# A mixture-of-experts layer behind a selective scan: the last shared block's start moved into the scan phase, the slot tables built in batches inside that block

## The chip, the cores and the metric

The kernel runs on one core of a Trainium2 chip. The metric is device microseconds of one execution, the median of several. Three runs of the kernel before gave 3494.13, 3504.29 and 3508.07 us. A core has TensorE (PE, with its weight load PEld), VectorE (DVE), ScalarE (ACT), GpSimd (POOL), SyncE (SP, which only issues DMAs here) and 16 DMA engines.

## The reference, cut to what matters

```python
x = x + layernorm(scan(layernorm(x)))          # 4096 rows of 512; softplus steps, state of 16
x = x + layernorm(moe(layernorm(x)))
def moe(xt):
    top_p, top_i = top_k(softmax(xt @ gate_w), 2)          # 8 experts
    for k in range(2):
        e, w = top_i[:, k], top_p[:, k]
        pos = (cumsum(one_hot(e), axis=0) - 1)[row, e]     # place of a token in its expert
        keep = pos < cap                                    # cap = 640
        buf[e, pos] = xt * keep
        y = gelu(buf @ w1 + b1) @ w2 + b2 + gelu(buf @ wd) @ wu
        out += y[e, pos] * keep * w
    return out + 0.2 * (gelu(xt @ sw1 + sb1) @ sw2 + sb2 + gelu(xt @ swd) @ swu)
```

Everything is in fp32. The large products run in the fp32r type, with each factor split into a high and a low part and three products (high-high, high-low, low-high) for one.

## The kernel before

The program has three phases with a barrier between them: `prepare` (projections and step sizes of the scan), `mix` (the scan), and `experts`.

In `mix` the work is placed by hand on a grid of units g, 64 per chunk of 512 rows, 8 chunks, and 64 more for the end (`END`). VectorE, ScalarE, GpSimd and TensorE each walk through all units and issue in each what is due then (`due(b, unit)` and the tuples `T_AT`, `X_HI_AT`, `X_LO_AT`, `UP_AT`, `DOWN_AT`). While the scan of a chunk runs, TensorE also does the shared expert of an earlier block of 512 rows: `turn` transposes four tiles of normalised rows, `x_hi` (ScalarE) and `x_lo` (VectorE) split them into `Xh` and `Xl`, up j=0 is the low-rank product with the logits in eight more columns, up and down of j=1 to 16 are the hidden layer in chunks of 128. `blocks(g)` yields the blocks that are under way, `FB` = 7 of the eight. In the 64 units after the scan only block 6's products are left. SP stores normalised rows (`xt_d`), logits (`lgT_d`) and the shared output.

`experts` has the eighth shared block (SB-1 = 7), and then eight experts of 10 tiles each, in blocks of 2, 4 and 4 tiles. A block is `run`: 17 chunks j, TensorE's order is up(j+1), a `turn` of the next block's tile at j in `FRONT`, extras, down(j). ScalarE applies GELU to up's result, VectorE makes its high part (`hh`, a copy) and low part (`hl`, a subtraction), down uses both. Beside it the next expert's weights come in: SP loads 256 KB pieces into a ring of four, ScalarE rounds them to the high part two chunks behind, when the old chunk's products are done, and GpSimd subtracts for the low part (`lows`, two operations a chunk), which frees the ring. The shared weights, split already in `mix`, are loaded by GpSimd in six `GROUPS` of four loads each; up(j) waits for its group.

Ahead of the shared block in `experts`, its rows are loaded, normalised, stored, turned and split one tile after another, the low-rank weights `L1` and `L2` are loaded and split again (`load_chunk(0, ...)`, `convert_chunk(0, 0)`, `lows(0, 0)`), and the logits of the first seven blocks are turned. The routing (softmax, two picks, cumulated counts by two products, places, table rows) runs on VectorE as `extra` steps in j = 1 to 12. After the block, `find_slots` fills the slot tables: for each of the 64 pairs (k, tile) VectorE makes a one-hot of the low 7 bits of the table row (128 columns) and one of the high bits times the token number (80 columns), and TensorE adds their product:

```python
v.tensor_scalar(low1[g % HOT], count_f[:, :], hl_f[:, 1, k, t:t + 1], None, ALU.is_equal)
v.tensor_scalar(high1[g % HOT], count_f[:, 0:E * ST], hl_f[:, 0, k, t:t + 1], tok_f[:, t:t + 1],
                ALU.is_equal, ALU.mult)
nc.tensor.matmul(psT[0][:, 0, 0:E * ST], low1[g % HOT], high1[g % HOT], start=(g == 0), stop=(g == K * NT - 1))
```

Then the table is copied, GpSimd gathers the first expert's two tiles of rows and its routing weights, TensorE turns them, and the first expert starts.

Of the kernel before, what the change touches and what calls it, by code (L numbers as in the profile page):

```python
# [24 lines left out]
P = 128  # L25
T, D = 4096, 512
NS, RANK = 16, 64
DT = D // P
# [342 lines left out]
W1_RING, W2_RING, HB_RING, HH_RING = 3, 3, 8, 4  # L371

# [6 lines left out]
def mix(nc, sem, const, early, x, dt_d, dtx_d, bc_d, xT_d, w, ws_d, lgT_d, x1_d, xt_d, sh_d):  # L379
# [6 lines left out]
    with ExitStack() as ctx:  # L386
# [13 lines left out]
        Xh, Xl = sb("Xh", [P, DT, CH], F32R), sb("Xl", [P, DT, CH], F32R)  # L400
        hh, hl = sb("hhs", [P, HH_RING, CH], F32R), sb("hls", [P, HH_RING, CH], F32R)
        L1h, L1l = sb("sL1h", [P, DT, P], F32R), sb("sL1l", [P, DT, P], F32R)
        L2 = sb("sL2", [L3, D], F32R)
# [3 lines left out]
        few = sb("b_few", [P, NU + FC + 14 * CT + 7 * CT])  # L407
# [34 lines left out]
        s_stat, s_pad, s_lhi, s_llo, s_l2 = (sem(f"b_{n}") for n in ("static_in", "pad", "low_hi", "low_lo", "low_up"))  # L442
# [33 lines left out]
        def blocks(g):  # L476

            return range(max(0, (g - FIRST) // NU - 3), min(FB, (g - FIRST) // NU))

# [9 lines left out]
        def _(sp):  # L489
# [63 lines left out]
            for g in range(END):  # L553
# [19 lines left out]
                if c > 0:  # L573
                    if k == 16:
                        store_x1(c - 1)
                    if c - 1 < FB and k in (20, 23, 29, 32):
                        store_xt(c - 1, (20, 23, 29, 32).index(k))
                for b in blocks(g):
                    for t in range(BT):
                        if due(b, OUT_AT) + 1 + t == g:  # L580
                            store_sh(b, t)
                    if due(b, UP_AT[0]) + 4 == g:
                        store_logits(b)
            sp.wait_ge(s_out, 16 * NCH)
            for q in range(2):
                sp.wait_ge(s_xt[q], FB * BT // 2 * 16)
            for t in range(BT):
                sp.wait_ge(s_sh[t], FB * 16)
            sp.wait_ge(s_lgs, FB * 16)

        @block.scalar
        def _(act):
# [94 lines left out]
            for g in range(END):  # L687
# [12 lines left out]
                if c > 0:  # L700
                    if k in (5, 6, 7, 8):
                        norm(c - 1, k - 5)
                    if c - 1 < FB and k in (18, 21, 27, 30):
                        norm_x1(c - 1, (18, 21, 27, 30).index(k))
                for b in blocks(g):
# [3 lines left out]
                    for j in range(J):  # L709
# [12 lines left out]
        def _(dve):  # L722
# [50 lines left out]
            def shared_out(b, t):  # L773
# [3 lines left out]
                if t >= 2:  # L777
                    dve.wait_ge(s_T, min(b + 2, FB) * BT)
                    dve.wait_ge(s_xt[t - 2], min(b + 2, FB) * (BT // 2) * 16)
# [15 lines left out]
            for g in range(END):  # L795
# [25 lines left out]
        def _(pool):  # L821
# [79 lines left out]
            nc.gpsimd.memzero(L1h[:, :, :]).then_inc(s_pad, 1)  # L901
            nc.gpsimd.memzero(L1l[:, :, :]).then_inc(s_pad, 1)
# [3 lines left out]
            for g in range(END):  # L906
# [14 lines left out]
                if 0 < c <= FB and k == 17:  # L921
# [8 lines left out]
        def _(pe):  # L930
# [28 lines left out]
            def up(b, j):  # L959
# [5 lines left out]
                else:  # L965
# [3 lines left out]
                    wh, wl = w1[n % W1_RING][:, 0, :, :], w1[n % W1_RING][:, 1, :, :]  # L969
                for d in range(DT):  # L970
                    for i, (a, v) in enumerate(((wh, Xh), (wh, Xl), (wl, Xh))):
                        last = nc.tensor.matmul(psH[:, :], a[:, d, :], v[:, d, :],  # L972
# [21 lines left out]
            for g in range(END):  # L994
# [4 lines left out]
                for b in blocks(g):  # L999
# [1143 lines left out]
```

## Time and profile before

| | us |
|---|---|
| median of three runs | 3504.29 |
| profiled execution | 3507.56 |
| its span | 3505.8 |
| TensorE busy | 3134.5 (89%) |
| VectorE, ScalarE, GpSimd busy | 1870.8, 1426.1, 1766.4 |
| TensorE's share of the chain that ended last | 53% |
| mean granted clock of TensorE | 0.935 |

A row of a timeline has a start, a duration, the engine, the line in the kernel and what was computed; matmuls are pipelined, so a single one lasts longer than the distance to the next. In square brackets stands how long the engine had been idle and who released it. The granted clock is 1.00 at 2.4 GHz and 0.50 at 1.2 GHz.

### The profile page before, as it was taken

How to read it: one execution, taken by the hardware profiler on the slowest of the kernel's cores; microseconds unless marked ns; L12 is line 12 of the kernel's file. 1: busy time of each engine (PE TensorE's matmuls, PEld its weight loads, DVE VectorE, ACT ScalarE, POOL GpSimd, SP SyncE). 2: the span in 40 equal slices, each digit the busy share in tenths (PEclk: the TensorE clock that was granted, in tenths of full speed). 3: DMA queues.
4: the chain of work that ended last, by engine and by line, in shares of the span. 5: the costliest groups of instructions: out<-in, count | busy, mean ns of one | idle time of the engine just before them, and what ended most of it. 6: DMA issues, size and time to landing. Idle time of an engine off the chain costs nothing.

```text
span 3505.8 us, 43215 instructions
## 1 busy us (share of the span) xinstructions
PE 3134.5 (89%) x15191; PEld 2569.3 (73%) x15191; DVE 1870.8 (53%) x2716; ACT 1426.1 (41%) x2522; POOL 1766.4 (50%) x1658
## 2 busy tenths in 40 slices
PE   6454698988989899689999999999999999999997
PEld 3233577777777777478888888888888888888886
DVE  6698989898898992373322322232223222322355
ACT  7555676666766764322231221321322312213232
POOL 1087797988878884342251341531522514405424
PEclk8655799999999999789999999999999999999999
DMA  7859687696977955821141230331322303304354
GB/s 256 250 173 239 180 238 207 198 259 192 249 194 219 244 174 168 263 85 40 43 102 22 69 79 16 97 64 19 112 36 55 90 19 79 76 10 108 79 181 153
DMA packets 279738, 467.63 MB, mean 133 GB/s; under 512 B 32321, under 2 KB 107985, under 8 KB 279522
## 3 DMA queue, kind: packets, MB, share of 16 engines
q1 hardware_dynamic: 211008, 274.60, 27.4%
q0 software_dynamic: 66752, 189.87, 20.8%
q8 instruction: 122, 2.00, 0.2%
q14 instruction: 94, 0.77, 0.1%
q10 hardware_dynamic: 1762, 0.40, 0.1%
HBM read 367.64 MB, written 97.14 MB: 133 GB/s over the span
## 4 chain that ended last, share of the span: by engine, by line
PE 53%; DMA 2%; DVE 2%; POOL 1%; issue 1%; ACT 1%; SPq 0%; POOLq 0%; DVEq 0%; ACTq 0%
PE c_psH L1959 26%; PE c_psY L2003 25%; PE c_psT L1950 1%; PE c_psT L2056 1%; DMA raw<-in_w 1%; PE c_psY L1999 0%; DMA out<-d_y 0%; DMA xrow<-x_d 0%; DVE yst L1673 0%; POOL W1l L1494 0%; DVE wgt L1850 0%; DVE hh L1683 0%; POOL W2l L1494 0%; ACT h L1409 0%; DVE hl L1684 0%
## 5 line engine op out<-in xcount | busy, mean ns | idle before, releaser
L1689 DVE CAST hh<-h 128x512 fp32r<-128x512 f32 (+1 forms) x400 | 180.4, 451 | 1178.0 <-ACT h L1415 1175.6
L829 POOL TENSOR_TENSOR u<-dtxs,Bt 128x512 f32<-128x512 f32 x512 | 669.6, 1343 | 162.7 <-DVE b_psA L732 148.9
L1415 ACT ACTIVATE h<-c_psH,biases 128x512 f32<-128x512 f32 (+1 forms) x400 | 248.2, 620 | 1222.1 <-PE c_psH L1959 1204.6
L732 DVE TENSOR_TENSOR_SCAN b_psA<-b_psA,b_few,u 128x512 f32<-128x512 f32 x512 | 657.0, 1283 | 58.8 <-ACT b_psA L602 55.7
L937 PE MATMUL b_psY<-ident,pr 128*128 128x128 f32 x2048 | 342.8, 305 | 221.8 <-DVE pr L739 202.4
L2003 PE MATMUL c_psY<-W2h,hh 128*128 128x512 f32 x1344 | 536.2, 399 | 4.3 <-DVE hl L1691 3.9
L2003 PE MATMUL c_psY<-W2l,hh 128*128 128x512 f32 x1344 | 527.0, 392 | 0.0
L2003 PE MATMUL c_psY<-W2h,hl 128*128 128x512 f32 x1344 | 525.8, 391 | 0.0
L1499 POOL DMA_INDIRECT xrow<-xt_d,slot_lists x80 | 91.1, 1139 | 817.9 <-PE c_psT L1950 417.1
L937 PEld LDWEIGHTS b_psY<-ident,pr 128*128 128x128 f32 x2048 | 262.3, 155 | 305.4 <-DVE pr L739 252.1
L739 DVE TENSOR_TENSOR pr<-b_psA,Ct 128x512 f32<-128x512 f32 x512 | 354.3, 692 | 20.4 <-DMA Ct<-bc_d 2.7
L602 ACT ACTIVATE b_psA<-dts,A_neg 128x512 f32<-128x512 f32 x512 | 354.3, 692 | 16.1
L1494 POOL TENSOR_TENSOR W1l<-raw,W1h 128x512 fp32r<-128x512 f32 x128 | 198.4, 1550 | 270.3 <-ACT W1h L1353 270.3
L972 PE MATMUL b_psH<-Xh,w 128*128 128x512 f32 x896 | 312.7, 410 | 9.8 <-DMA w<-ws_d 9.8
L2003 PEld LDWEIGHTS c_psY<-W2h,hh 128*128 128x128 f32 x1344 | 254.2, 189 | 57.2 <-DVE hl L1691 9.5
L991 PE MATMUL b_psS<-w,hhs 128*128 128x512 f32 x896 | 294.7, 411 | 0.0
L2003 PEld LDWEIGHTS c_psY<-W2h,hl 128*128 128x128 f32 x1344 | 253.7, 189 | 55.2
L2003 PEld LDWEIGHTS c_psY<-W2l,hh 128*128 128x128 f32 x1344 | 254.4, 189 | 46.9 <-issue 0.2
L1691 DVE TENSOR_TENSOR hl<-h,hh 128x512 fp32r<-128x512 f32 (+1 forms) x400 | 252.7, 632 | 13.8
L1959 PE MATMUL c_psH<-Xbh,W1h 128*128 128x512 f32 x576 | 224.7, 390 | 0.0
L1959 PE MATMUL c_psH<-Xbh,W1l 128*128 128x512 f32 x576 | 224.2, 389 | 0.0
L1959 PE MATMUL c_psH<-Xbl,W1h 128*128 128x512 f32 x576 | 224.1, 389 | 0.0
(278 smaller groups left out, 5792.7 us busy)
## 6 DMA issues: line engine op xcount, KB each, us to landing
w<-ws_d POOLq DMA_DIRECT2D x224, 512.0 KB, 6.7
raw<-in_w SPq DMA_DIRECT2D x256, 256.0 KB, 2.7
Bt<-bc_d SPq DMA_DIRECT2D x64, 512.0 KB, 15.1
Ct<-bc_d SPq DMA_DIRECT2D x64, 512.0 KB, 19.1
xn<-in_x SPq DMA_DIRECT2D x8, 1024.0 KB, 7.0
xT_d<-xnT SPq DMA_DIRECT2D x8, 1024.0 KB, 8.6
dt_d<-a_dt SPq DMA_DIRECT2D x8, 1024.0 KB, 7.2
dtx_d<-a_dx SPq DMA_DIRECT2D x8, 1024.0 KB, 7.6
```

Source lines behind the costliest of these rows:

```text
L602: nc.scalar.activation(psA[g % 2][:, :], dts[s % 2][:, :], ACT.Exp, scale=A_neg[:, s % DT, n:n + 1]).then_inc(s_dA, 1)
L732: nc.vector.tensor_tensor_scan(psA[q][:, :], psA[q][:, :], u[g % U_RING][:, :], carry[:, k:k + 1], ALU.mult, ALU.add).then_inc(s_h, 1)
L739: nc.vector.tensor_tensor(pr[g % PR_RING][:, :], psA[g % 2][:, :], C_of(g), ALU.mult)\
L829: nc.gpsimd.tensor_tensor(u[g % U_RING][:, :], dtx[s % 2][:, :], Bt[n // TG][:, n % TG, :], ALU.mult)\
L937: last = nc.tensor.matmul(psY[:, t, :], pr[g % PR_RING][:, t * P:(t + 1) * P], ident[:, :], start=(n == 0 and t == 0), stop=False, is_tran ...
L972: last = nc.tensor.matmul(psH[:, :], a[:, d, :], v[:, d, :], start=(d == 0 and i == 0), stop=(d == DT - 1 and i == 2))
L991: last = nc.tensor.matmul(psS[t][:, :], a, v, start=False, stop=(j == FC and i == 2))
L1415: nc.scalar.activation(h32[:, 0:n * P], psH[j % 2][:, 0:n * P], ACT.Gelu, bias=b1[:, j - 1:j]).then_inc(s_gelu, 1)
L1494: nc.gpsimd.tensor_tensor(lo, view, hi.bitcast(F32), ALU.subtract).then_inc(s_wlo, 1)
L1691: nc.vector.tensor_tensor(hl[j % 2][a], h32[a], hh[j % 2][a].bitcast(F32), ALU.subtract)\
L1959: last = nc.tensor.matmul(out, a, b, start=(i == 0), stop=(i == n - 1))
L2003: last = nc.tensor.matmul(psY[t][:, :], a[j % 2][:, c], b, start=False, stop=(j == J - 1 and i == 2))
```

## The change

The eighth block's rows are normalised, stored, turned and split in `mix`, in the 64 units behind the scan, and its up 0 is done there for the logits (`turned(g)`, one block further than `blocks(g)`). `Xh`, `Xl`, `L1` and `L2` are allocated once for both phases and stay; `L1` has 104 columns in `mix` too and is not cleared any more. `experts` starts with up 0 of the shared block; the bias and logits transpositions stand between up 0 and up 1 (`lead`). GpSimd issues the loads of the first two groups first, then its constants, then the other loads. The routing is spread over j = 0 to 7; the sums over tiles are one scan of 512 elements with resets in place of 16 scans of 32. The one-hots are built in eight batches of eight tiles by tensor_tensor operations into fp32r tiles, two batches in each of j = 8 to 11, and TensorE adds them in j = 9 to 12. The slots are found in j = 12; GpSimd gathers the first expert's rows before its low parts of chunks 10 to 16, and TensorE turns them in j = 14 and 15 (`FRONT_0`). The weights of the routing are stored in j = 10.

```diff
+        def turned(g):
+            return range(max(0, (g - FIRST) // NU - 1), min(FB + 1, (g - FIRST) // NU))
...
-                    if c - 1 < FB and k in (18, 21, 27, 30):
+                    if k in (18, 21, 27, 30):
                         norm_x1(c - 1, (18, 21, 27, 30).index(k))
-                for b in blocks(g):
+                for b in turned(g):
                     for t in range(BT):
                         if due(b, X_HI_AT[t]) == g:
                             x_hi(b, t)
-                    for j in range(J):
+                    if due(b, UP_AT[0]) + 2 == g:
+                        hidden_out(b, 0)
+                for b in blocks(g):
+                    for j in range(1, J):
...
-            nc.gpsimd.memzero(L1h[:, :, :]).then_inc(s_pad, 1)
-            nc.gpsimd.memzero(L1l[:, :, :]).then_inc(s_pad, 1)
...
-                for b in blocks(g):
+                for b in turned(g):
                     for t in range(BT):
                         if due(b, T_AT[t]) == g:
                             turn(b, t)
+                    if due(b, UP_AT[0]) == g:
+                        up(b, 0)
+                for b in blocks(g):
                     for j in range(J):
-                        if due(b, UP_AT[j]) == g:
+                        if j > 0 and due(b, UP_AT[j]) == g:
                             up(b, j)
...
-FRONT = (2, 6, 10, 14)
-HOT = 4
+FRONT, FRONT_0 = (2, 6, 10, 14), (14, 15)
+BATCH = 8
+BATCHES = K * NT // BATCH
+BATCH_AT = 8
...
+        low1 = sb("low_one_hot", [P, 2, BATCH, P], F32R, rt)
+        high1 = sb("high_one_hot", [P, 2, BATCH, E * ST], F32R, rt)
...
+            for b in range(SB):
+                sp.dma_start(logits_in(b), lgT_d[:, b * BT * P:(b + 1) * BT * P]).then_inc(s_lin, 16)
             sp.dma_start(b2bc[:, :], w["sb2"].partition_broadcast(P)).then_inc(s_b2, 16)
-            sp.dma_start(graw[:, :, :], w["gate"].rearrange("(a p) e -> p a e", p=P)).then_inc(s_gin, 16)
-            for b in range(SB - 1):
-                sp.dma_start(old_logits(b), lgT_d[:, b * BT * P:(b + 1) * BT * P]).then_inc(s_lin, 16)
-            rows(SB - 1)
             sp.wait_ge(s_bt, 2)
-            load_chunk(0, SHARED_W, 0)
...
-            nc.scalar.activation(rs1[:, :], mv1[:, :, 1], ACT.Sqrt, bias=eps[:, :]).then_inc(s_sd, 1)
-            act.wait_ge(s_pad, 2)
-            act.wait_ge(s_gin, 16)
-            nc.scalar.copy(L1h[:, :, L3:L3 + E], graw[:, :, :]).then_inc(s_ghi, 1)
-            act.wait_ge(s_nm, 1)
-            for t in range(BT):
-                normalise(SB - 1, t)
-                x_hi(shared(SB - 1), 1, None, t)
 ...
-            run(shared(SB - 1), b1T[:, E * FC:], logits=True, wset=1, extra={2: (exponentials,)})
...
-            act.wait_ge(s_wst, K * 16)
-            for t in range(EB[0][1]):
-                x_hi(expert(0, 0), X_OF[0], None, t)
+            def store_weights():
+                act.wait_ge(s_wT, 1)
+                nc.scalar.copy(weight_rows, psT[1][0:K * NT, 0, :]).then_inc(s_wTc, 1)
+                act.wait_ge(s_wTc, 1)
+                for k in range(K):
+                    act.dma_start(w_d[k].rearrange("(r p) o -> r (p o)", p=P), weight_rows[k * NT:(k + 1) * NT, :])\
+                        .then_inc(s_wst, 16)
+            run(shared(SB - 1), b1T[:, E * FC:], nxt=(expert(0, 0), X_OF[0], None), front=FRONT_0, wset=1, extra={1: (exponentials,), BATCH_AT + 2: (store_weights,)})
...
+            for k in range(2):
+                load_shared(k)
+            nc.gpsimd.memset(wsl[:, :], SHARE).then_inc(s_share, 1)
...
+            nc.gpsimd.memset(fresh.rearrange("p (x t) -> p x t", t=NT)[:, :, 0:1], 0.0).then_inc(s_rc, 1)
+            for k in range(2, len(GROUPS)):
+                load_shared(k)
+            for j in range(BATCH_AT + 2):
                 lows(1, j)
-            for q in range(2):
-                pool.wait_ge(s_xts[q], BT // 2 * 16)
             slots_known(0)
             gathers(0, 0, range(2))
             pool.wait_ge(s_wst, K * 16)
             gather_weights(0, 0)
+            for j in range(BATCH_AT + 2, J):
+                lows(1, j)
             gathers(0, 1, range(2))
...
+            def sums():
+                step(v.tensor_tensor_scan(RA[:, :, :, :].rearrange(flat), fresh, RB[:, :, :, :].rearrange(flat), 0.0,
+                                          ALU.mult, ALU.add))
...
+            def one_hots(i):
+                k, r = i * BATCH // NT, slice(i * BATCH % NT, i * BATCH % NT + BATCH)
+                low, high = low1[:, i % 2, :, :], high1[:, i % 2, :, :]
+                def spread(a, n):
+                    return a.unsqueeze(2).to_broadcast([P, BATCH, n])
+                def counts(n):
+                    return count_f[:, 0:n].unsqueeze(1).to_broadcast([P, BATCH, n])
+                dve.wait_ge(s_rows, 1)
+                after(dve, s_add, i - 1)
+                v.tensor_tensor(high, counts(E * ST), spread(hl_f[:, 0, k, r], E * ST), ALU.is_equal).then_inc(s_heq, 1)
+                v.tensor_tensor(low, counts(P), spread(hl_f[:, 1, k, r], P), ALU.is_equal).then_inc(s_low, 1)
+                dve.wait_ge(s_heq, i + 1)
+                v.tensor_tensor(high, high.bitcast(F32), spread(tok_f[:, r], E * ST), ALU.mult).then_inc(s_high, 1)
             def find_slots():
-                dve.wait_ge(s_rows, 1)
-                for g in range(K * NT):
-                    k, t = g // NT, g % NT
-                    after(dve, s_add, g - HOT + 1)
-                    v.tensor_scalar(low1[g % HOT], count_f[:, :], hl_f[:, 1, k, t:t + 1], None, ALU.is_equal)\
-                        .then_inc(s_low, 1)
-                    v.tensor_scalar(high1[g % HOT], count_f[:, 0:E * ST], hl_f[:, 0, k, t:t + 1], tok_f[:, t:t + 1],
-                                    ALU.is_equal, ALU.mult).then_inc(s_high, 1)
-                dve.wait_ge(s_add, K * NT)
+                dve.wait_ge(s_add, BATCHES)
...
+            routing = {0: (less_max,), 2: (probabilities, lambda: pick(0)), 3: (lambda: mark(0),),
+                       4: (lambda: pick(1), lambda: mark(1)), 5: (totals, sums), 6: (places,), 7: (table_rows,)}
+            for i in range(0, BATCHES, 2):
+                routing[BATCH_AT + i // 2] = (lambda i=i: one_hots(i), lambda i=i: one_hots(i + 1))
+            routing[BATCH_AT + BATCHES // 2] = (find_slots,)
...
+            def biases_and_logits():
+                pe.wait_ge(s_bin, 32)
+                nc.tensor.transpose(psT[0][:, 0, :], raw[0][:, 0:P], ident[:, :]).then_inc(s_bt, 1)
+                nc.tensor.transpose(psT[1][:, 0, 0:FC], raw[1][0:FC, 0:P], ident[0:FC, 0:FC]).then_inc(s_bt, 1)
+                pe.wait_ge(s_lin, SB * 16)
...
+                last.then_inc(s_lT, 1)
...
-            run(shared(SB - 1), 1, 0, logits=True, extra={8: cumulate})
-            pe.wait_ge(s_rows, 1)
-            nc.tensor.transpose(psT[1][0:K * NT, 0, :], wgt[:, :, :].rearrange("p k t -> p (k t)"), ident[:, :])\
-                .then_inc(s_wT, 1)
-            for g in range(K * NT):
-                pe.wait_ge(s_low, g + 1)
-                pe.wait_ge(s_high, g + 1)
-                nc.tensor.matmul(psT[0][:, 0, 0:E * ST], low1[g % HOT], high1[g % HOT],
-                                 start=(g == 0), stop=(g == K * NT - 1)).then_inc(s_add, 1)
-            pe.wait_ge(s_wTc, 1)
-            for t in range(EB[0][1]):
-                turn(expert(0, 0), t)
+            def turn_weights():
+                pe.wait_ge(s_rows, 1)
+                nc.tensor.transpose(psT[1][0:K * NT, 0, :], wgt[:, :, :].rearrange("p k t -> p (k t)"), ident[:, :])\
+                    .then_inc(s_wT, 1)
+            def add_slots(i):
+                pe.wait_ge(s_low, i + 1)
+                pe.wait_ge(s_high, i + 1)
+                for o in range(BATCH):
+                    last = nc.tensor.matmul(psT[0][:, 0, 0:E * ST], low1[:, i % 2, o, :], high1[:, i % 2, o, :],
+                                            start=(i == 0 and o == 0), stop=(i == BATCHES - 1 and o == BATCH - 1))
+                last.then_inc(s_add, 1)
+            steps = {5: (cumulate,), BATCH_AT: (turn_weights,)}
+            for i in range(0, BATCHES, 2):
+                steps[BATCH_AT + 1 + i // 2] = (lambda i=i: add_slots(i), lambda i=i: add_slots(i + 1))
+            steps[FRONT_0[0] - 1] = (lambda: pe.wait_ge(s_wTc, 1),)
+            run(shared(SB - 1), 1, 0, lead=biases_and_logits, nxt=expert(0, 0), front=FRONT_0, extra=steps)
...
+            def kept_tile(name, shape, dt=F32R, where=ctx):
+                return where.enter_context(nc.sbuf_tensor(name, shape, dt, side="right"))
+            kept_tile("edge", [P, 16], F32)
+            const["L1"] = [kept_tile(f"L1{h}", [P, DT, L3 + E]) for h in "hl"]
...
+            const["L2"] = kept_tile("L2", [L3, D])
+            const["X"] = [kept_tile(f"X{h}", [P, DT, CH]) for h in "hl"]
```

## Rows read from the trace of the kernel before

**Rows 1.** Four stages: engines' busy us (count), granted clock, DMA share, GB/s.

```profile
1442.90:1539.10 96.20, 96.18 (x409) 77.39 (x409) 51.17 (x87) 35.44 (x60) 53.90 (x49) 0.97 0.79 240
1539.10:1580.40 41.30, 29.90 (x138) 28.64 (x137) 33.40 (x138) 2.68 (x6) 9.73 (x10) 0.56 0.12 35
1580.40:1631.80 51.40, 51.36 (x319) 46.73 (x320) 16.49 (x43) 11.41 (x23) 10.89 (x13) 0.95 0.16 51
1816.80:1868.70 51.90, 49.74 (x320) 44.70 (x319) 19.06 (x44) 12.76 (x26) 20.91 (x18) 1.00 0.33 67
```

**Rows 2.** The chain that ended last, in order of time: start us, us, what.

```profile
1458.13 2.72 PE c_psH L1959 x12
```

**Rows 3.** Timeline between the phases: start us, us, engine, line, operation.

```profile
1402.51 0.39 PE L991 MATMUL b_psS<-w,hls 128*128 128x512 f32 x1
...
1409.56 0.11 POOL L1545 MEMSET slot_lists<- 128x10 f32 x1 [11.44 <-POOLq L2124]
...
1414.92 0.59 POOL L1566 DMA_DIRECT2D W1h<-ws_d  x1
...
1442.82 0.75 POOL L1566 DMA_DIRECT2D W1h<-ws_d  x1
...
1453.86 0.80 POOL L1568 DMA_DIRECT2D W2l<-ws_d  x1
```

**Rows 4.** Timeline of TensorE, start of the shared block.

```profile
1442.92 0.76 PE L1959 MATMUL c_psH<-Xbh,L1h 128*104 128x512 f32 x1 [5.17 <-POOL L L1494]
...
1448.17 0.55 PE L1959 MATMUL c_psH<-Xbh,W1h 128*128 128x512 f32 x1
...
1452.52 0.39 PE L1959 MATMUL c_psH<-Xbh,W1h 128*128 128x512 f32 x1
```

**Rows 5.** Timeline of the scan phase: clearing a tile, turning a tile of rows.

```profile
171.51 0.53 POOL L901 MEMSET sL1h<- 128x512 uint32 x1
...
1256.31 0.60 PE L956 MATMUL b_psH<-ident,xn 128*128 128x128 f32 x4
```

**Rows 6.** DMA issues, from 1417 and from 1445.6 us: KB each, us to landing.

```profile
W2l<-ws_d POOLq DMA_DIRECT2D x2, 256.0 KB, 6.4
...
W2l<-ws_d POOLq DMA_DIRECT2D x1, 1024.0 KB, 15.0
```

**Rows 7.** Timeline of ScalarE and TensorE at the first converted chunk.

```profile
1466.71 0.62 ACT L1353 CAST W1h<-raw 128x512 fp32r<-128x512 f32 x1 [5.13 <-DMA raw<-in_w]
...
1468.68 0.68 ACT L1415 ACTIVATE h<-c_psH,biases 128x512 f32<-128x512 f32 x1
...
1471.57 0.39 PE L2003 MATMUL c_psY<-W2h,hh 128*128 128x512 f32 x1
```

**Rows 8.** VectorE groups with shapes, 1400 to 1600 us: count, busy us, mean ns.

```profile
L1808 DVE TENSOR_SCALAR xrow<-U,RA 128x128 f32<-128x128 f32 x64 | 18.5, 290 | 0.0
...
L1741 DVE TENSOR_TENSOR RB<-RB,w 128x256 f32<-128x256 f32 x2 | 0.9, 426 | 0.1
...
L1763 DVE TENSOR_TENSOR RA<-RA,RB 128x512 f32<-128x512 f32 x1 | 0.7, 684 | 0.0
```

**Rows 9.** Timeline of GpSimd and VectorE, a collision and a free pair.

```profile
1504.05 1.47 POOL L1494 TENSOR_TENSOR W2l<-raw,W2h 128x512 fp32r<-128x512 f32 x1
...
1504.41 1.66 DVE L1691 TENSOR_TENSOR hl<-h,hh 128x512 fp32r<-128x512 f32 x1
...
1523.57 0.43 DVE L1689 CAST hh<-h 128x512 fp32r<-128x512 f32 x1 [1.41 <-ACT h L1415]
1524.03 0.69 DVE L1691 TENSOR_TENSOR hl<-h,hh 128x512 fp32r<-128x512 f32 x1
```

**Rows 10.** Timeline of GpSimd and TensorE, the first expert's rows.

```profile
1572.76 1.16 POOL L1499 DMA_INDIRECT xrow<-xt_d,slot_lists  x1 [29.83 <-issue]
...
1577.77 1.12 PE L1950 MATMUL c_psT<-ident,xrow 128*128 128x128 f32 x4 [0.32 <-DMA xrow<-xt_d,slot_lists]
...
1590.07 0.60 PE L1950 MATMUL c_psT<-ident,xrow 128*128 128x128 f32 x4
```

More of the change, by code:

```diff
@@ L798, in _ @@
                     static_lo()
-                for b in blocks(g):
+                for b in turned(g):
                     for t in range(BT):
@@ L998, in _ @@
                         add_skip(g // NS)
-                for b in blocks(g):
+                for b in turned(g):
                     for t in range(BT):
@@ L1673, in leave, with run @@
                 nc.vector.scalar_tensor_tensor(out, psY[t][:, :], scale, out, ALU.mult, ALU.add).then_inc(s_yev, 1)
-            def run(at, logits=False, nxt=None, extra=None, late=None, leaves=True):
+            def run(at, nxt=None, extra=None, late=None, leaves=True, front=FRONT):
                 G, n = at["B"] * J, at["n"]
@@ L1961, in products, with run @@
                 return last
-            def run(at, xb, s, logits=False, nxt=None, extra=None, final=False):
+            def run(at, xb, s, lead=None, nxt=None, extra=None, final=False, front=FRONT):
                 G, n = at["B"] * J, at["n"]
@@ L1990, in down @@
                     if j == 0:
-                        if logits:
+                        if lead:
                             pe.wait_ge(s_lg, 4)
@@ L2009, in run @@
                 up(0)
+                if lead:
+                    lead()
                 for j in range(J):
@@ L2012, in run @@
                         up(j + 1)
-                    if logits and j == 0:
-                        pass_gate(pe, s_lT, at["B"] + 1, g_pe)
-                        for t in range(BT):
-                            last = nc.tensor.transpose(psH[0][:, t * E:(t + 1) * E],
-                                                       h32[L3:L3 + E, t * P:(t + 1) * P], ident[L3:L3 + E, L3:L3 + E])
-                        last.then_inc(s_lP, 1)
-                    if nxt and j in FRONT and FRONT.index(j) < nxt["n"]:
-                        t = FRONT.index(j)
+                    if nxt and j in front and front.index(j) < nxt["n"]:
+                        t = front.index(j)
@@ L2021, in run @@
                         turn(nxt, t)
                     if extra and j in extra:
-                        extra[j]()
+                        for part in extra[j]:
+                            part()
                     down(j)
-            for t in range(BT):
-                turn(shared(SB - 1), t)
-            pe.wait_ge(s_bin, 32)
-            nc.tensor.transpose(psH[0][:, 0:P], raw[0][:, 0:P], ident[:, :]).then_inc(s_bt, 1)
-            nc.tensor.transpose(psH[1][:, 0:FC], raw[1][0:FC, 0:P], ident[0:FC, 0:FC]).then_inc(s_bt, 1)
@@ L2059, in _ @@
-            for t in range(EB[0][1]):
-                turn(expert(0, 0), t)
+                pe.wait_ge(s_rc, 7 + E)
+                pe.wait_ge(s_b1, 2)
+                picked = OH[:, :, :, :].rearrange(flat)
+                nc.tensor.matmul(psT[0][:, :, :].rearrange("p a b -> p (a b)"), U[:, :], picked, start=True, stop=True)
+                nc.tensor.matmul(psT[1][:, :, :].rearrange("p a b -> p (a b)"), ones[:, :], picked,
+                                 start=True, stop=True).then_inc(s_cum, 1)
```

253 lines of the change are left out of this document (90 added, 163 removed).

## Prediction

> **What bounds the kernel now.** I read the chain of waits first. It is TensorE for half of the span, and inside the shared block and the expert blocks it is nothing else: twelve products take 2.72 us [rows 2], so a chunk j (one up, one down) takes 5.44 us, and every other engine waits for it. The two places where TensorE does not work are seen in the table of stages and in the timeline between the phases. The last product of the scan phase starts at 1402.51, the experts phase starts at 1409.56, and its first product only at 1442.92 [rows 3, 4]: the last shared block's rows are loaded, normalised, turned and split there first. After that block come 41.3 us [rows 1] in which TensorE is paced by VectorE: 64 pairs of one-hots, one pair per product, then the slots are copied, the first expert's rows gathered and turned, and at 1580.38 the first expert starts. The granted clock shows the same: 0.97 and 1.00 in the blocks, 0.56 in this gap. From there to the end TensorE is full (49.74 of 51.9 us even in a block with a boundary). So the change is worth what it removes between 1402.5 and 1580.4, less what it adds to TensorE or makes TensorE wait for.
>
> **The change, part by part.** S is the first instruction of the experts phase on GpSimd (1409.56 before); I count from it.
>
> 1. Start of the scan phase: two clearings of 0.53 us [rows 5] go, and they stand ahead of the first product for the scan on GpSimd. -1.0 (0 to -1.0).
>
> 2. End of the scan phase: eighth block. Its four tiles of rows are turned there (4 x 0.60 us [rows 5]) and the low-rank product with the logits done (2.72): +5.1 on TensorE, which is full there. ScalarE and VectorE get four normalisations, four high and four low copies, SP four row stores and one of logits; both engines mostly wait in this stretch, and the order by units places each turn one down product after the copies it waits for. I count no stall; a missed slot each time would be about 1 us, so +4.6 to +9. S becomes 1409.56 - 1.0 + 5.1 = 1413.7.
>
> 3. Start of the experts phase: loading, normalising, turning and the low-rank weights' loading are gone; weights and rows lie in SBUF. Up 0 starts at once, at the low clock: in the trace twelve products took 1442.92 to 1448.17 = 5.25 us and then the clock rose [rows 4]. What is late next is data. The biases and eight logits pieces must land (ten issues on SP, which feed 34 small transposes), and up 1 needs the first weights: their fourth issue is some 1.6 us after S, and such a load lands 6.4 us after issue [rows 6], so S+8. Up 1 takes 2.7 to 5.25 by the clock, down 0 another 1.0: the third up starts at S+11.7 to S+14.3. I take S+13.
>
> 4. Weight supply. GpSimd issues eight loads, about 3 us of constants (an estimate, those of before and two more), then sixteen loads (11.8 us before, 1442.82 to 1454.6 [rows 3]), so from S+7.3 to S+19.1. Before, the last load of the group for j=5 to 8 was issued at 1447.9 and took 15.0 us [rows 6], 20 us after the first of the sixteen: S+27.4. TensorE wants it after the third up plus six half chunks, S+13+16.3=S+29.3. No stall, with 1.9 us to spare. The expert's own chunks are tighter. Before, GpSimd was done with its issues 2.1 us after the third up's start; now 6.1 us after. It then had waited for ScalarE until 1458.2, so only some 1.5 us of the 4 come through. The first converted chunk waited 5.13 us for its load, the next GELU came at 1468.68, and the down product that uses it started at 1471.57 [rows 7]; the two VectorE steps between end about 0.4 us ahead. 1.5 - 0.4 gives +1.0 (0 to 3).
>
> 5. The routing and the batches. From the third up to the end of the block took 1452.52 to 1538.9 = 86.4 us [rows 4, 1], the two cumulating products included; that stays. The routing steps only move by some chunks, under the same cover. New on TensorE are 64 products of 128x80 in j=9 to 12. The trace has none in this type. By columns from 0.227 us for 512 it is 0.035 each, 2.3 in all; the nearest other, a 128x128 transposition, is 0.15 busy [rows 5], 9.6 in all. I take 0.09 each: +5.8. Two turns of the expert's rows inside: +1.0.
>
> VectorE now computes 8 batches of three operations, 640, 1024 and 640 elements. From 426 ns for 256 and 684 ns for 512 elements [rows 8] it is 168 ns + 1.01 ns per element: 0.81 + 1.20 + 0.81 = 2.8 us a batch, 5.7 us a chunk. Its own pair for the block is 0.43 + 0.69. But GpSimd makes two low halves per chunk, and while one runs, a VectorE operation with two SBUF inputs stands still: the low half of h took 1.66 us beside such a GpSimd operation and 0.69 without [rows 9]. That is 1 us per low half, 2 per chunk. VectorE's chunk is 1.1 + 5.7 + 2.0 = 8.8 us, TensorE's 5.44 + 1.45 = 6.9 us. Four chunks give 7.6 us; VectorE has about a half chunk of lead at the start. +6 (0 to 14). The double buffer doesn't bind: a batch waits for the product of the one two before it, which in the same chunk comes earlier.
>
> The Trainium skill ("SBUF — State Buffer", Who interferes with whom) says that a VectorE instruction with two SBUF inputs and a GpSimd instruction that reads SBUF exclude each other for the whole instruction. The trace agrees with 1.66 against 0.69 us [rows 9]. By full exclusion of the 2.6 us of two low halves the chunk would be 9.4 us and the forecast 2 us later, 3454.
>
> The skill's "VectorE: DVE Perf Modes" (The perf-mode tier table) speaks against this edit: a tensor_scalar in fp32 has a double rate from SBUF, a tensor_tensor has not, and the batches change from the one to the other. At 128 elements the trace shows 290 ns for tensor_scalar [rows 8], nearly all of it fixed, so per element the batch is the cheaper one here.
>
> 6. End of the shared block. Slots known just after the adds of j=12; 1572.76 to 1577.77 are 5.0 us from the first gather to the second tile's turning [rows 10], and turn 0 stands 11 us behind in TensorE's queue: hidden. But GpSimd now does the low halves of seven chunks (14 x 1.3 us) after these gathers, and behind them the gathers for the second block. Next in its queue stand row stores, weights and those gathers. The last low half needs the last down product, then some 4 us; gather and landing 3.5 us; TensorE turns that tile 9.7 us after the expert's start (1580.38 to 1590.07). +0.5 (0 to 5). The expert's first block then is like a later one with its boundary, 51.9 instead of 51.4 us [rows 1]: +0.5.
>
> **Sum.** Before, S to the expert's start: 1580.38 - 1409.56 = 170.8. After: 13 + 86.4 + 1.0 + 5.8 + 6 + 1.0 = 113.2. That is -57.6; with -1.0, +5.1 and +1.0 it is -52.5. The profiled execution has 3505.8 us of span and 3507.56 in all, 3.3 above the median of 3504.29. So 3455.1 by that execution, 3451.8 by the median: **3452 us**, 1.5% faster. All terms at their good end give 3439, all at their bad end (+25) 3477.
>
> **Rivals.**
> - VectorE decides more than I count: operands repeated along a dimension run at half rate. Nothing in the trace repeats both inputs of one operation. A chunk would be 1.1 + 11.3 + 2.0 = 14.4 against 6.9, 30 us instead of 6: 3476.
> - Weight supply. The shared weights are 16.8 MB; the block moved 240 GB/s on average [rows 1]. At that rate the 8.4 MB up to j=8 last 35 us and TensorE stands 6 us: 3458. Against it: 1024 KB loads then landed in 15.0 us with three others ahead of them.
> - The end of the block: GpSimd's queue, in which the second block's gathers stand behind 14 low halves, makes TensorE wait at the tile turned in j=2, or ScalarE's late conversions hold a GELU, 5 us: 3457. This is also how the change would not do all that it says.
> - The other side: the clock. TensorE now starts the block cold, with pauses for logits and weights. If these keep it at the lower level (0.437 us a product in up 0 against 0.227) through the block's 400 products, that is +84: 3536, slower than before. It decides if the clock is still 0.5 after j=3. Against it: it rose 5.25 us after the first product, and before that TensorE had been idle even longer.
>
> **How the numbers follow.** Forecast 0.68, VectorE 0.10, supply 0.09, block's end 0.08, clock 0.03, no gain for a reason I don't see 0.02. The range, 3439 to 3475, holds the forecast with its terms, the supply, the block's end and most of the first rival. A measurement of this kernel tells about 0.5% (17.5 us) from no change: faster 0.95 (everything up to 3487), within 0.02, slower 0.03.
>
> **What would show it.** Right: last product of the scan phase 4 to 5 us later; first product of the experts within 0.5 us of S; third up at S+13 and clock 1.00 from there; no TensorE wait at j=3 and j=5; chunks j=8 to 11 at 7 to 9 us with VectorE nearly full; no gap at the end of the block, and the first expert about 53 us earlier (near 1527); all later blocks as before. Wrong: a weights wait on TensorE, batches' operations above 1.5 us with GpSimd idle, a late clock, or a block of the experts that is longer than its 51.9 us.

## The result, and the profile after

| | before | changed | difference |
|---|---|---|---|
| time, median (range), us | 3504.36 (3494.13 to 3508.07) | 3459.52 (3457.46 to 3466.31) | ratio 0.988 (0.9855 to 0.9905) |
| span of the profiled execution, us | 3505.8 | 3455.7 | -50.1 |
| first expert's first product after S, us | 170.8 | 121.7 | -49.1 |

The forecast was 3452 with a range of 3439 to 3475; the kernel came out 7.5 us slower than forecast. The sign, the place and six sevenths of the gain (44.8 of 52.3 us) are right. The difference of the two spans, 50.1 us, holds 3.9 us that are the luck of the profiled execution (experiment 1). What the single parts bring is read from the profiles; only the last part, the early gathers, was also taken back by itself (experiment 4).

The stages of the changed kernel, columns as in [rows 1]: start to third up, to the batches, the batches, to the end of the block, the first expert's first block.

```profile
1409.30:1423.80 14.50, 11.26 (x63) 8.42 (x63) 3.09 (x10) 1.68 (x5) 14.41 (x37) 0.67 1.03 281
1423.80:1470.80 47.00, 46.22 (x199) 36.69 (x198) 33.04 (x51) 19.55 (x32) 24.24 (x22) 1.00 1.21 371
1470.80:1502.30 31.50, 30.01 (x150) 25.56 (x149) 28.58 (x30) 7.64 (x14) 8.91 (x6) 0.89 0.19 60
1502.30:1531.00 28.70, 24.56 (x106) 19.94 (x106) 14.88 (x16) 7.55 (x14) 18.21 (x16) 0.94 0.37 103
1531.00:1582.10 51.10, 49.48 (x319) 44.52 (x318) 18.64 (x44) 12.76 (x26) 16.14 (x17) 1.00 0.22 67
```

The 41.3 us at clock 0.56 of [rows 1] are gone, and so are the 33 us before the first product [rows 3, 4]. What is not as forecast is seen in lines three and four: the clock is 0.89 and 0.94 where it was 1.00, and in line four TensorE is busy 24.56 of 28.70 us. TensorE's timeline at the start, against [rows 4]; a bracket is idle time and what ended it:

```profile
1408.94 0.73 PE L1915 MATMUL c_psH<-Xh,L1h 128*104 128x512 f32 x1 [6.26 <-PEq L2097]
...
1416.91 0.63 PE L1985 MATMUL c_psY<-ident,OH 8*128 8x8 f32 x16 [3.24 <-DMA RB<-lgT_d]
...
1417.92 0.80 PE L1915 MATMUL c_psH<-Xh,W1h 128*128 128x512 f32 x1
...
1423.76 0.40 PE L1915 MATMUL c_psH<-Xh,W1h 128*128 128x512 f32 x1
```

S is 1409.32. The first product stands 0.4 us ahead of it, the logits land at S+7.6, up 1 starts at S+8.6 and takes 4.9 us, ten of its products at the low level (0.427 us apart), and the third up starts at S+14.4.

The chain of waits of the changed kernel, in its own order of time (start us, us, what). Of [rows 2] only TensorE stood there; now there are gaps between TensorE's stretches:

```profile
1420.77 19.53 DMA W2l<-ws_d
1440.34 3.04 PE c_psH L1915 x12
...
1486.56 1.91 DVE high_one_hot L1775
1488.47 1.83 DVE high_one_hot L1772
1490.37 0.99 issue
1491.36 0.82 DVE high_one_hot L1775
1492.32 1.06 PE c_psT L2010 x8
1493.38 4.53 PE c_psY L1957 x12
...
1508.70 8.43 DVE hh L1647
1517.90 4.60 PE c_psY L1957 x12
1522.50 2.72 PE c_psH L1915 x12
```

The weights for j=5 land at 1440.3, S+31, just as TensorE asks for them: it stands 0.23 us. The load took 19.5 us. In the batches VectorE decides. And one cast of VectorE lasts 8.43 us where 0.43 is usual [rows 9]. Behind it, and behind the batches, twelve down products take 4.6 and 4.53 us instead of 2.72. The timeline of VectorE and GpSimd around that cast:

```profile
1502.38 0.24 DVE L1780 COPY slot_rows<-c_psT 128x80 f32<-128x80 f32 x1 [2.86 <-PE c_psT L2010]
...
1504.22 1.16 POOL L1460 DMA_INDIRECT xrow<-xt_d,slot_lists  x1 [14.60 <-issue]
...
1508.36 1.01 POOL L1485 DMA_INDIRECT slot_lists<-w_d,slot_lists  x1 [0.30 <-issue]
...
1508.70 8.42 DVE L1647 CAST hh<-h 128x512 fp32r<-128x512 f32 x1 [3.68 <-ACT h L1386]
...
1509.39 1.29 POOL L1455 TENSOR_TENSOR W1l<-raw,W1h 128x512 fp32r<-128x512 f32 x1
...
1515.58 1.25 POOL L1455 TENSOR_TENSOR W2l<-raw,W2h 128x512 fp32r<-128x512 f32 x1
...
1517.15 0.69 DVE L1649 TENSOR_TENSOR hl<-h,hh 128x512 fp32r<-128x512 f32 x1
...
1517.90 0.76 PE L1957 MATMUL c_psY<-W2h,hh 128*128 128x512 f32 x1 [4.14 <-DVE hl L1649]
```

GpSimd stood from 1489.6 to 1504.2 for the slots, with the low halves of expert chunk 10 (converted by 1495.0) and 11 (by 1502.4) behind the gathers in its queue. Then six low halves run without a gap, 1509.39 to 1516.83, and the cast that should end at 1509.1 ends at 1517.12.

**How the experiments are read.** The kernel before had medians of 3504, 3504, 3514 and 3505 us in the four groups of runs, and in the thirteen profiles the last scan started anywhere from 1328 to 1348 us. Effects of a few us are therefore read from S to the first expert's first product (S+121.7 above); repeats agree within 0.7 us. lows3, fewadds4 and equaltwice4 ran once each. From the last scan to S it is 80.13 to 80.18 us in every profile with the change and 75.45 before.

### The profile page after: what moved, and what is told of

Its sections match the earlier page's. It is cut to its first block, busy times and chain, and to the rows that moved or that the text cites. A ratio compares the mean times of both kernels' runs of the same rounds, so it can differ in the third digit from the quotient of the medians.

```text
span 3455.7 us, 42915 instructions
## 1 busy us (share of the span) xinstructions
PE 3128.9 (91%) x15139; PEld 2558.6 (74%) x15139; DVE 1862.4 (54%) x2594; ACT 1421.4 (41%) x2514; POOL 1763.8 (51%) x1655
## 4 chain that ended last, share of the span: by engine, by line
PE 51%; DVE 3%; DMA 2%; POOL 1%; issue 1%; ACT 1%; POOLq 0%; DVEq 0%; SPq 0%; ACTq 0%
PE c_psH L1915 25%; PE c_psY L1957 24%; PE c_psT L1906 1%; DMA raw<-in_w 1%; DMA W2l<-ws_d 1%; PE c_psY L1953 0%; DVE yst L1631 0%; DVE hh L1647 0%; POOL W1l L1455 0%; DVE wgt L1809 0%; DMA out<-d_y 0%; DVE hh L1641 0%; POOL W2l L1455 0%; DVE high_one_hot L1775 0%; ACT h L1384 0%
## 5 line engine op out<-in xcount | busy, mean ns | idle before, releaser
L836 POOL TENSOR_TENSOR u<-dtxs,Bt 128x512 f32<-128x512 f32 x512 | 665.0, 1328 | 160.7 <-DVE b_psA L738 142.4
L942 PE MATMUL b_psY<-ident,pr 128*128 128x128 f32 x2048 | 350.2, 310 | 206.7 <-DVE pr L745 188.8
L1915 PE MATMUL c_psH<-Xh,W1h 128*128 128x512 f32 x576 | 225.5, 392 | 0.1
L1915 PE MATMUL c_psH<-Xl,W1h 128*128 128x512 f32 x576 | 225.0, 391 | 0.0
L1915 PE MATMUL c_psH<-Xh,W1l 128*128 128x512 f32 x576 | 224.9, 390 | 0.0
```

The lines of the kernel that those rows point to most:

```text
L836: nc.gpsimd.tensor_tensor(u[g % U_RING][:, :], dtx[s % 2][:, :], Bt[n // TG][:, n % TG, :], ALU.mult)\
L942: last = nc.tensor.matmul(psY[:, t, :], pr[g % PR_RING][:, t * P:(t + 1) * P], ident[:, :], start=(n == 0 and t == 0), stop=False, is_tran ...
L1915: last = nc.tensor.matmul(out, a, b, start=(i == 0), stop=(i == n - 1))
```

## Experiments

**1. after_again**, no edit.

> The changed kernel once more, unaltered. Counted from S, the experts phase's first instruction on GpSimd, the first expert started at S+121.8 in its profile, against S+113.2 forecast. My theory of the miss: (a) six low halves in a row on GpSimd (7.5 us) held VectorE's cast of hidden chunk 14 for 8.4 us and TensorE for 4.1 us; (b) TensorE's clock fell to the lower level after each wait in the batches and after that stall, 5.0 us together. If so both are back here in the same places: expert at S+120 to S+123, total 3455 to 3465 us. Rival: the 8.4 us was a one-off of that execution (a late load); then the expert starts at S+116 and the total is 3454. Second question: in the profiled execution the scan phase gained 3.9 us more than its 1.1 us at the start, in small steps. If the gain belongs to the change (the moved turns and normalisations), the last scan starts again 4.5 to 5.5 us earlier than the 1334.1 of before; if it was chance of one execution, 0 to 3 us earlier or later.

Ratio 0.988 (0.9864 to 0.9897), 3459.85 us, first expert at S+121.0. The cast again:

```profile
1512.68 8.42 DVE L1647 CAST hh<-h 128x512 fp32r<-128x512 f32 x1 [3.68 <-ACT h L1386]
```

Same place, same length: no one-off. The last scan starts at 1333.85, as before the change (1334.11; 1329.17 in the first profile). The extra 3.9 us were that execution's luck. The first scan starts 1.1 us earlier than before in both, as much as the two clearings took; but in the twelve profiles with the change it starts anywhere from 171.8 to 174.8 us (173.9 before), so that this gain is not shown.

**2. lows4 and 3. lows3.** Two chunks' low halves, or one chunk's, ahead of the gathers:

```diff
-            for j in range(BATCH_AT + 2):
+            for j in range(BATCH_AT + 4):      # lows3: + 3
                 lows(1, j)
             slots_known(0)
             gathers(0, 0, range(2))
 ...
-            for j in range(BATCH_AT + 2, J):
+            for j in range(BATCH_AT + 4, J):
```

> The changed kernel with the low halves of expert chunks 10 and 11 ahead of the first expert's gathers in GpSimd's queue instead of behind them. Pile-up theory: GpSimd waits for the slots from 1489.6 to 1504.2 with chunk 10 ready at 1495.0 and chunk 11 at 1502.4; with both done ahead of the gathers only two low halves stand in a row afterwards, the cast of chunk 14 takes under 3 us, TensorE's 4.1 us stall and the 1.6 us of low clock behind it go: first expert at S+116.1, total 5.7 us below the changed kernel. The batches of chunk 11 get two low halves beside them (+2 us on VectorE, which has 2 us to spare there): 0 to +1. Rival A: the four indirect gathers (1504.2 to 1509.4), not the low halves, hold VectorE's cast; then it stays at 8 us and the time is unchanged. Rival B: something else is late next, the gathered rows (gathers 0.3 to 1 us later, turn 0 has some 3 us to spare) or the raw pieces; then the gain is 0 to 3 us.

> Dose between the two: only chunk 10's low halves stand ahead of the gathers, so four stand in a row behind them (5.1 us instead of 7.5). Pile-up theory: the cast of chunk 14 takes about 5.5 to 6 us instead of 8.4, TensorE waits 1.5 us instead of 4.1, clock falls or not: first expert at S+117 to S+119.5, total 2.5 to 4.5 us below the changed kernel. Rival A (gathers hold the cast): 8.4 us as before, S+121.8.

lows4: 3454.23 us against 3459.85 for the unaltered kernel on the same chip, ratio 0.9871 (0.9854 to 0.9889), S+115.4 (115.6 when repeated as lows4_again). lows3: 3457.14 us, S+117.5. The cast in lows3, then the same cast in lows4, and TensorE's wait in lows3:

```profile
1516.68 5.87 DVE L1647 CAST hh<-h 128x512 fp32r<-128x512 f32 x1 [3.79 <-ACT h L1386]
```

```profile
1509.27 0.43 DVE L1647 CAST hh<-h 128x512 fp32r<-128x512 f32 x1 [1.68 <-ACT h L1386]
1509.56 1.02 POOL L1485 DMA_INDIRECT slot_lists<-w_d,slot_lists  x1 [0.30 <-issue]
```

With six in a row the cast takes 8.42 us, with four 5.87 us, and each time it ends 0.3 us after the last low half of the row. The four gathers are the same in both, so they do not set the length (Rival A falls). In lows4 the cast starts between two gathers and is over before any low half starts. TensorE's wait goes from 4.14 over 1.60 to none. The medians differ by 5.6 us where 5.7 were expected, but the single times of the two kernels overlap (3449.55 to 3464.73 and 3457.28 to 3464.47); the landmark carries it, S+115.4 and S+115.6 against S+121.7 and S+121.0.

A row of low halves alone is not enough, however. In the trace before, a cast starts inside a row of four and is held for one low half only, and the next operation for one more; GpSimd's own operations get longer in turn:

```profile
1495.57 1.31 POOL L1494 TENSOR_TENSOR W2l<-raw,W2h 128x512 fp32r<-128x512 f32 x1
1495.69 1.46 DVE L1689 CAST hh<-h 128x512 fp32r<-128x512 f32 x1 [2.76 <-ACT h L1415]
1496.83 1.47 POOL L1494 TENSOR_TENSOR W1l<-raw,W1h 128x512 fp32r<-128x512 f32 x1
1497.19 1.66 DVE L1691 TENSOR_TENSOR hl<-h,hh 128x512 fp32r<-128x512 f32 x1
```

In the thirteen profiles 79 casts of this shape start inside a low half with at least one more directly behind it; the longest took 1.59 us. The three long ones (after, after_again, lows3) are the only casts that start beside a gather with a row of low halves directly behind it. As far as these runs go, it takes both: the start beside the last gather, ahead of the row, and the row. Why the cast does not end there, no run shows.

**4. gathers_late.** The change's last part undone: no `nxt` in the shared block's `run` on all three engines, the two tiles turned and split behind it, and on GpSimd:

```diff
+            for j in range(J):
+                lows(1, j)
             slots_known(0)
             gathers(0, 0, range(2))
             pool.wait_ge(s_wst, K * 16)
             gather_weights(0, 0)
```

> The changed kernel with its last part undone: the first expert's gathers stand behind all low halves in GpSimd's queue, and its two tiles are turned and split behind the shared block, not inside it. Pile-up theory: no low halves pile up, so the stall of 4.1 us and 1.6 us of clock go, and 1.1 us of turns leave the block (S+115 at its end); then the last low half, 5.0 us from first gather to turn and 4.0 us from turn to product (both measured before the change) give the first expert at S+124 to S+126: 2 to 4 us above the changed kernel. Rival A (gathers hold VectorE wherever they run): the block ends at S+115 as well, so this one does not tell them apart; it prices the part: by my prediction's own terms 8 to 9 us, by the theory 3 us net of the stall that the part brings along. Rival C (the part is worth nothing since GpSimd is behind anyway): the same time as the changed kernel.

3463.96 us, ratio 0.9896 (0.9879 to 0.9912), S+126.4, just outside what was expected; no cast of the block takes more than 1.6 us. The price is in one line:

```profile
1530.67 1.12 PE L1908 MATMUL c_psT<-ident,xrow 128*128 128x128 f32 x4 [7.82 <-DMA xrow<-xt_d,slot_lists]
```

So this part brings 11.0 us (126.4 - 115.4) with the queue in good order and 5 us as it was made (126.4 - 121.7).

**5. fewadds4 and 6. equaltwice4.** Who is the limit in the batches? Both on lows4: fewer products on TensorE, or more work on VectorE.

```diff
-                for o in range(BATCH):
+                for o in (0, BATCH - 1):
```

```diff
                 v.tensor_tensor(high, counts(E * ST), ..., ALU.is_equal).then_inc(s_heq, 1)
+                dve.wait_ge(s_heq, 2 * i + 1)
+                v.tensor_tensor(high, counts(E * ST), ..., ALU.is_equal).then_inc(s_heq, 1)
```

> lows4 (which starts the first expert at S+115.4) with 16 of the 64 slot products: six of eight in each batch are left out, so the slots are incomplete; VectorE's work is the same. The products take 0.106 us each in the trace, 48 of them 5.1 us of TensorE. Theory: in chunks 8 to 11 VectorE is the limit (8.46 us a chunk without one idle gap, TensorE 7.15), so TensorE only waits longer for the same batches: expert at S+113.5 to S+115. Rival: TensorE is the limit there and the waits of 0.5 to 0.95 us are small change: expert at S+110.3 or earlier.

> lows4 with the first operation of each batch (the high one-hot, 0.74 us from start to start) done twice: VectorE gets 8 x 0.74 = 5.9 us more, with more time lost beside GpSimd's low halves up to 9. VectorE as the limit: expert at S+121.5 to S+124.5. TensorE as the limit: S+115.4 to S+117.5.

fewadds4: S+115.3 (3456.25 us), nothing gained from 5.1 us less on TensorE. equaltwice4: S+123.7 (3484.27 us, where the kernel before took 3513.5), 8.3 us more. VectorE is the limit. Of the 8.3 us, 6.8 are VectorE's: its cast behind the last batch starts at S+98.1, in lows4 at S+91.4. The other 1.5 us are products at the low level in the down behind that batch, which lows4 did not have; the expectation of half4 below puts all 8.3 down to VectorE's work. TensorE in fewadds4, waiting for a batch and then for the hidden chunk:

```profile
1480.74 0.39 PE L2010 MATMUL c_psT<-high_one_hot,low_one_hot 128*128 128x80 f32 x2 [1.60 <-DVE high_one_hot L1775]
1481.71 0.50 PE L1957 MATMUL c_psY<-W2h,hh 128*128 128x512 f32 x1 [0.58 <-DVE hl L1649]
```

**7. split4.** The second batch's products behind the down product (also on lows4):

```diff
                    down(j)
+                    if behind and j in behind:
+                        behind[j]()
```

> lows4 with the second batch of each chunk added behind the chunk's down product instead of ahead of it. The three waits for the second batch (0.94, 0.55, 0.95 us) and the low clock behind the first of them (1.4 us) go, but VectorE's last batch is ready no earlier (1501.7 in lows4's profile); of the 2.7 us of down 12 that now lie ahead of it 2.7 us come back: expert at S+112.7 (112 to 113.5), total 2.7 us below lows4. Rival: the waits only move to the first batch of each chunk and the clock falls there as well: S+114 to S+115.5. Rival on the clock: it falls because of the narrow products themselves, wait or no wait: then there are low stretches behind batches that came without a wait; in the five profiles so far there is none.

A miss: 3467.21 us, S+117.7, 2.3 us worse than lows4 where 2.7 better was expected; ratio 0.9871 (0.9853 to 0.9889), which does not tell the two apart. I had read VectorE's order wrongly. It makes batches i and i+1, then the hidden chunk's halves: whenever `down` may start, batch i+1 has long been ready. Its products used to fill TensorE's wait for `hl`; moved behind, they leave it open (waits of 1.91, 0.29, 0.97 and 0.99 us for `hl` ahead of the downs) and are added to the path.

**8. tokensplit4.** split4, with the product of one-hot and token number on ScalarE:

```diff
-                v.tensor_tensor(high, high.bitcast(F32), spread(tok_f[:, r], E * ST), ALU.mult)...
+                for o in range(BATCH):
+                    nc.scalar.activation(a, a.bitcast(F32), ACT.Copy, scale=tok_f[:, r:r + 1])...
```

> split4 with the third operation of each batch (high one-hot times token number) taken from VectorE and done on ScalarE, eight products of 128x80 by a column of scales per batch. VectorE's chunk falls from 8.46 us by 1.5 (without GpSimd beside it) to 3.8 us (with), so to 4.7 to 7; ScalarE's rises from 2.6 us by 16 x 0.24 (its 128x128 copy takes 0.27, its 128x16 copy 0.18) to 6.5. TensorE's 7.15 us is then the longest: no wait for a batch, no low clock between 1470 and 1505: expert at S+111.5 (110.5 to 112.5), 1 us below split4. Rival: ScalarE is late with a GELU since it stands waiting for the high one-hots: S+113 to S+118.

3482.77 us, S+130.9, ratio 0.9907 (0.9892 to 0.9922): the rival, larger than it was given. ScalarE works its queue in order:

```profile
1492.51 2.13 ACT L1416 ACTIVATE high_one_hot<-high_one_hot,tok_f 128x80 fp32r<-128x80 f32 x8 [2.99 <-DVE high_one_hot L1782]
1496.62 2.13 ACT L1416 ACTIVATE high_one_hot<-high_one_hot,tok_f 128x80 fp32r<-128x80 f32 x8 [1.99 <-DVE high_one_hot L1782]
1498.66 0.60 ACT L1335 CAST W1h<-raw 128x512 fp32r<-128x512 f32 x1
1499.17 0.61 ACT L1335 CAST W2h<-raw 128x512 fp32r<-128x512 f32 x1
1499.69 0.68 ACT L1386 ACTIVATE h<-c_psH,biases 128x512 f32<-128x512 f32 x1
```

The GELU of the next chunk stands behind the second batch, that one behind a buffer that comes free only with products behind the down. The down products of j=9 to 12 start 10.8, 13.0 and 13.4 us apart.

**9. half4 and 10. full4**, both batches ahead of the down again: half4 gives ScalarE the first batch of each pair, full4 both, behind its conversions. **11. lows4_again** beside them.

> lows4 (second batch ahead of the down product again) with the third operation of every other batch, the first of each chunk, on ScalarE. What the last four runs say: VectorE is the limit in chunks 8 to 11 (48 products fewer changed nothing, 8.3 us more VectorE work cost 8.3 us), and ScalarE takes 0.26 us for each product of a one-hot with its token numbers, 2.1 us a batch. VectorE's chunk falls by 0.74 us, or by 1.8 where a low half stood beside that operation: 8.46 to about 7.2, TensorE's is 7.15, ScalarE's 0.6 + 1.3 + 2.1 + 1.2 = 5.2. VectorE theory: 4 x 1.2 = 4 to 5 us with the clock's share, first expert at S+110.5 to S+112 (lows4: S+115.4), total 3 to 5 us below lows4. Rival: what ScalarE does in between delays the GELU as in the run before, S+116 or more.

> lows4 with the third operation of all batches on ScalarE, behind its conversions of the chunk, not ahead of them, and both batches ahead of the down product. VectorE's chunk is then 1.1 + 4 x 0.93 = 4.8 us and up to 2 us more beside low halves, TensorE's 7.15, ScalarE's 0.6 + 2.0 (to the first high one-hot) + 4.2 = 6.8, or 8 to 8.8 where low halves delay the second batch. If ScalarE keeps under TensorE: S+110.5 to S+112, like the half. If it is the new limit, 1 to 1.5 us in each of four chunks: S+114 to S+117. I hold the second for likelier. It also says what made the run before slow: its split adds (each batch's buffer came free only behind a down product, ScalarE waited for it with the next GELU behind) or ScalarE's work; in the first case this one is far below S+130.9.

> lows4 unaltered, beside the two on the same chip: first expert at S+115 to S+116 (S+115.4 before), ratio to the kernel before 0.9855 to 0.9885.

| | ratio to before | first expert |
|---|---|---|
| half4 | 0.9865 (0.9848 to 0.9881) | S+112.7 |
| full4 | 0.9867 (0.985 to 0.9883) | S+117.5 |
| lows4_again | 0.9867 (0.985 to 0.9883) | S+115.6 |

By the profile half4 is 2.9 us better than lows4_again, just short of what was expected, and has no low clock in the batches. full4 is 1.9 us worse. Some 1.2 us of that stand ahead of the batches, where weights came 2.4 us late (down 7 starts at S+54.4, in lows4_again at S+53.2). In the batches ScalarE is the limit, as held likelier: VectorE's casts stand 8.5 to 8.8 us apart, and each time it waits 1.7 to 2.6 us for `h`. By the times the three are the same (medians 3459.41, 3459.58 and 3458.69 us); half4 is the fastest version only as far as S to the first expert tells. half4 and full4 lie 18 and 13 us below tokensplit4. full4 gives ScalarE the same multiplications, so most of that one's loss was not their amount; whether it was the split adds or their place ahead of the conversions is open, since full4 changed both.

## Why the prediction was right, and where it was off

| step | forecast | measured |
|---|---|---|
| 1. start of the scan phase | -1.0 | -1.1, within the scatter (-2.1 to +0.9) |
| 2. end of the scan phase | +5.1 | +4.7 |
| 3. S to third up | 13 | 14.4 |
| 4. weights, at j=5 and at the first converted chunk | 0 and +1.0 | 0.2 and 0 |
| 5. third up to the end, without what follows | 86.4 | 86.6 |
| 5. slot products | 5.8 | 6.8 (0.106 each) |
| 5. VectorE late, routing and batches | 6 | 0.7 + 1.5 of waits, 3.0 of low clock |
| 6. turns in the block | 1.0 | 0.7 |
| 6. end of the block | 0 (to 5) | 4.1 of wait, 1.4 of low clock |
| the rest, mostly first products late after pauses | 0 | 2.3 |
| S to the first expert | 113.2 | 121.7 |

Step 2 held; step 1 is too small to tell. Step 4 came out by luck: the weights for j=5 landed at S+31.0, not S+27.4, since their load took 19.5 us and not 15.0, and they held TensorE up for only 0.2 us because it was itself 1.4 us late; on the forecast's own times (it asks at S+29.3) it would have waited 1.7 us. Step 3 missed by 0.6 us of late start of up 1 (S+8.6) and by the clock: I had 2.7 to 5.25 us for up 1 and took a value between; it took 4.9. Step 5 was right in mechanism and nearly in size: VectorE's casts of hidden chunks stand 8.46 us apart in three of the four chunks (8.8 forecast; 6.3 in the last, which has no low halves beside it), its operations take 0.82, 1.22 and 0.82 us (0.81, 1.20, 0.81 forecast), half rate on repeated operands is refuted, and experiments 5 and 6 show that VectorE is the limit there. TensorE falling to the low level at a wait was left out; in the batches part of it cost nothing, since VectorE was late anyway. That waits and low clock add up to 5.2 where 6 us of waits were forecast is in part luck.

**The step that failed is step 6.** It saw that seven chunks' low halves stand behind the gathers, and asked only who waits for them. It priced the end of the block at +0.5 us (0 to 5) and counted no wait of TensorE inside the block; TensorE stood 4.1 us there, and the low clock behind that cost 1.4 us more. It did not ask what the low halves do when they come all at once. I had priced GpSimd against VectorE as 1 us per low half, because in [rows 9] one low half delays one operation. That price is right for an operation that starts while low halves run; experiments 2 and 3 show that a cast that starts beside the last gather is held until the whole row behind it is over. And I counted only operations with two SBUF inputs, though the trace before has casts of 1.4 to 1.5 us beside low halves (1495.69, 1502.96, 1509.09), which I passed over. The third rival, "the end of the block", had the queue and the size (5 us, 3457) but another victim: no gather was late.

The Trainium skill ("SBUF — State Buffer", Who interferes with whom) lists copy and cast among the operations that can take the pair of ports shared with GpSimd, and says that whoever issues first has it "for the whole instruction". The first part agrees with the casts above and would have widened my term. The second agrees with the row of four in the trace before, where the two engines took turns. It does not cover the long cast, which started 0.7 us ahead of the first low half and yet ended behind the sixth.

Of the rivals, VectorE at half rate and the clock staying low did not happen. The supply rival was near: 0.2 us of wait here, up to 2.7 us in the other profiles.

## What to carry to other kernels

When a new wait is put into an in-order queue, count what piles up behind it and what the pile can do to its neighbours when it runs off, not only who waits for its results; here it was cheaper to let the part of the pile that is ready run before the wait (lows4). To learn which of two engines is the limit, take work from one and give work to the other: the two answers (0.1 and 8.3 us) leave no doubt, where moving work about misled me twice. When the whole time scatters by more than the effect, measure between two landmarks in the profile that bracket the change.

## What the runs showed of the hardware

- A cast of 128x512 on VectorE, both sides in SBUF, that started beside a gather on GpSimd took 8.42 us (twice) and 5.87 us with six and four low halves directly behind that gather. The other 273 casts of this shape that started beside an indirect DMA of GpSimd in the thirteen profiles took 0.42 to 0.66 us, and the 79 that started inside a row of low halves at most 1.59 us. What stays open: in the held cases it had started 0.6 to 0.7 us ahead of the first low half and yet had not ended.
- The granted clock fell to the low level after TensorE's wait of 0.93 to 0.94 us between the two batches of chunk 9 in each of the six profiles of kernels with that order and the full products (after, after_again, lows3, lows4, lows4_again, gathers_late), for 6 to 8 products and 1.2 to 1.6 us. After the waits of 0.5 to 0.6 us in chunk 11 it fell in one of the six, after those of 0.9 us in chunk 12 (four of the six have one) in none, and never after batches that came without a wait. The first products at the low level, of the changed kernel:

```profile
1475.40 1.06 PE L2010 MATMUL c_psT<-high_one_hot,low_one_hot 128*128 128x80 f32 x8 [0.94 <-DVE high_one_hot L1775]
...
1477.30 0.63 PE L1957 MATMUL c_psY<-W2h,hh 128*128 128x512 f32 x1
```

- ScalarE took 2.13 us for eight 128x80 products with a column of scales (tokensplit4), start to start 0.26 each, more than VectorE's 0.82 us for all 640 elements a partition in one operation.
